# Layer 0 attention: the probabilities times v as fp32 matmuls, v kept in fp32, low halves of rows and attention made on GpSimd

## What is computed

```
def _L0_xattn_ref(q, k, v, w_q, b_q, w_k, b_k, w_v, b_v, w_o, b_o):
    qh = _split_heads(q @ w_q.T + b_q)
    kh = _split_heads(k @ w_k.T + b_k)
    vh = _split_heads(v @ w_v.T + b_v)
    scores = jnp.einsum('bhqd,bhkd->bhqk', qh, kh) / jnp.sqrt(jnp.float32(d_k))
    attn = jax.nn.softmax(scores, axis=-1)
    out = jnp.einsum('bhqk,bhkd->bhqd', attn, vh)
    return out.transpose(0, 2, 1, 3).reshape(B, S, H * d) @ w_o.T + b_o

x = x + jnp.tanh(g_xattn[0]) * _L0_xattn_ref(_layernorm(x, axis=-1), ctx_1024, ctx_1024, ...)
```

## Time and profile before

| | |
|---|---|
| median of 3 runs | 3130.3 us (3129.72 to 3131.92) |
| span of the profiled execution, first to last instruction | 3124.2 us |
| median less that span | 6.1 us |
| TensorE busy, matmul / weight load | 2797.3 us (90%) / 2225.3 us (71%) |
| VectorE, ScalarE, GpSimd busy | 2640.9 us (85%), 1875.0 us (60%), 2190.1 us (70%) |
| projection stage, about | 0 to 525 us |
| attention of layer 0, about | 527 to 1325 us |

### The profile page before, as it was taken

The page is one execution under the profiler, slowest core; times in us unless marked ns, Lnnn a source line. Parts: engine busy times, 40 slices in busy tenths (PEclk is TensorE's granted clock), DMA queues, the critical chain, the costliest instruction groups (busy, mean ns, idle before and its releaser), DMA issues.

```text
span 3124.2 us, 101333 instructions
## 1 busy us (share of the span) xinstructions
PE 2797.3 (90%) x33450; PEld 2225.3 (71%) x33450; DVE 2640.9 (85%) x6703; ACT 1875.0 (60%) x3733; POOL 2190.1 (70%) x3924
## 2 busy tenths in 40 slices
PE   4889896788888888869899999999999999999997
PEld 2444444666666666647688888888888888888886
DVE  6887886888888888875699999998989988999986
ACT  2666765777777777775455545555545555555553
POOL 3892001666667666645488888888888888888887
PEclk9999998999999999989999999999999999999999
DMA  5987666232223222623444444444444344444441
GB/s 153 361 332 289 244 243 227 73 86 79 73 78 83 80 74 77 224 82 81 96 104 111 107 101 95 104 104 95 101 91 97 94 103 104 96 98 93 108 94 43
DMA packets 367621, 388.79 MB, mean 124 GB/s; under 512 B 118432, under 2 KB 341264, under 8 KB 362320
## 3 DMA queue, kind: packets, MB, share of 16 engines
q1 hardware_dynamic: 346960, 335.42, 38.9%
q0 software_dynamic: 7328, 23.40, 2.4%
q10 hardware_dynamic: 12960, 25.23, 2.2%
HBM read 235.08 MB, written 148.83 MB: 123 GB/s over the span
## 4 chain that ended last, share of the span: by engine, by line
PE 39%; DVE 6%; issue 3%; POOL 2%; ACT 2%; DVEq 0%; POOLq 0%; ACTq 0%
PE banks L150 11%; PE banks L152 11%; PE banks L151 10%; PE banks L1310 2%; PE banks L1295 2%; DVE a_probT_lo L1397 1%; PE banks L1342 1%; ACT a_qT_hi L1199 1%; DVE a_pick L1522 1%; DVE a_y L1541 1%; DVE a_rsum L1409 1%; PE banks L1365 1%; DVE a_wsel L1531 0%; PE banks L1357 0%; ACT a_ynT_hi L1199 0%
## 5 line engine op out<-in xcount | busy, mean ns | idle before, releaser
L1199 ACT ACTIVATE a_qT_hi<-banks 128x512 f16<-128x512 f32 x252 | 150.5, 597 | 700.8 <-PE banks L152 700.8
L383 POOL TENSOR_TENSOR a_probT_lo<-a_expT,a_probT_hi 128x512 f16<-128x512 f32 (+1 forms) x384 | 372.0, 998 | 243.7 <-ACT a_probT_hi L458 243.7
L449 ACT ACTIVATE a_expT<-banks,a_top,w_score_scale 128x512 f32<-128x512 f32 (+1 forms) x384 | 272.2, 709 | 111.4 <-PE banks L544 111.2
L1112 POOL TENSOR_TENSOR a_pn<-a_prob,a_rsum 128x1024 f32<-128x1024 f32 (+1 forms) x256 | 307.2, 1221 | 5.8 <-DVE a_rsum L1411 5.3
L150 PE MATMUL banks<-a_xnT_hi,w_q_hi 128*128 128x256 f16 x1024 | 281.6, 275 | 4.7 <-DVE a_xnT_lo L1395 3.0
L150 PE MATMUL banks<-a_vo_front,a_probT_hi 128*128 128x256 f16 x1024 | 278.9, 272 | 2.7 <-DVE a_probT_lo L1397 2.6
L152 PE MATMUL banks<-a_xnT_hi,w_q_lo 128*128 128x256 f16 x1024 | 280.9, 274 | 0.0
L151 PE MATMUL banks<-a_xnT_lo,w_q_hi 128*128 128x256 f16 x1024 | 280.9, 274 | 0.0
L152 PE MATMUL banks<-a_vo_front,a_probT_lo 128*128 128x256 f16 x1024 | 279.0, 273 | 0.0
L151 PE MATMUL banks<-a_vo_front,a_probT_hi 128*128 128x256 f16 x1024 | 279.0, 272 | 0.0
L1397 DVE SCALAR_TENSOR_TENSOR a_probT_lo<-banks,a_probT_hi 128x512 f16<-128x512 f32 (+1 forms) x384 | 212.6, 582 | 35.7 <-ACT a_probT_hi L1199 35.3
(11 more groups left out here) (400 smaller groups left out, 10655.0 us busy)
## 6 DMA issues: line engine op xcount, KB each, us to landing
vo<-kv_vo_out SPq DMA_DIRECT2D x38, 2048.0 KB, 7.6
a_vo_front<-vo SPq DMA_DIRECT2D x128, 512.0 KB
kt<-kv_k_out ACTq DMA_DIRECT2D x9, 2560.0 KB, 15.0
a_k<-kt SPq DMA_DIRECT2D x64, 308.0 KB, 3.5
kv_raw_e<-in_L_ffn_w POOLq DMA_DIRECT2D x16, 1024.0 KB, 9.7
a_x<-in_x SPq DMA_DIRECT2D x64, 256.0 KB
a_y<-in_x SPq DMA_DIRECT2D x64, 256.0 KB, 2.8
x<-a_y SPq DMA_DIRECT2D x64, 256.0 KB, 2.2
```

The source lines that it names most:

```text
L383: pool.tensor_tensor(probT[b][1][0:rows, first:end, :], expT[b][0:rows, first:end, :], probT[b][0][0:rows, first:end, :], ALU.subtract).th ...
L449: act.activation(expT[1 - h][0:rows, first:end, :], bank, ACT.Exp, bias=top[0:rows, 0:1], scale=weights["score_scale"][0:rows, 0:1]).then_ ...
L1112: last = pool.tensor_tensor(keys_of(pn[h]), keys_of(prob_of(u, h, 2)), rsum[h][:, :].unsqueeze(2).broadcast_to([P, H, n]), ALU.mult)
L1199: act.activation(out, bank[:, 0:cols].rearrange("p (c s) -> p c s", c=out.shape[1]), ACT.Copy, scale=scale)\
```

## The change

v of layer 0 is stored in fp32, 17 values for a head (16 and a one) instead of 33 fp16; in the projection stage one VectorE addition writes it, and v_sum, the high copy and the low subtraction go. In attend the exponentials, fp32 and without the factor 16384, are the stationary operand of one fp32 matmul for each of the 10 chunks; the copies, the low halves on GpSimd, the bank's clearing by a zero matmul and the tile of zeros go. The buffers of the exponential are now free when the tile's att is ready. xnT and attT are evicted by ScalarE twice, in fp32 (xnT_full, attT_full) and in fp16, and GpSimd makes the low halves from these two in SBUF; VectorE's two subtractions go. Their banks are free after ScalarE's second eviction. q is still split by ScalarE and VectorE.

```diff
-    front = [sb(f"front{p}", [P, 2, 2, MAIN, 2 * head + 1], F16) for p in range(2)]
-    back = [sb(f"back{p}", [MAIN * BACK, 2, 2, MAIN, 2 * head + 1], F16) for p in range(2)]
+    front = [sb(f"front{p}", [P, 2, 2, MAIN, head + 1]) for p in range(2)]
+    back = [sb(f"back{p}", [MAIN * BACK, 2, 2, MAIN, head + 1]) for p in range(2)]
...
         if what == "xnT":
-            return xnT_ready, (i + 1) * DC + h + 1
+            return xnT_hi, (i + 1) * DC + h + 1
...
         if what == "attT":
-            return attT_ready, t - 2
+            return attT_hi, t - 2
...
-        def prob_lo(t, b):
...
+        def rows_lo(i, part):
+
+            need(pool, xnT_hi, (i + 1) * DC + part + 1)
+            pool.tensor_tensor(xnT[1][:, part, :], xnT_full[:, part, :], xnT[0][:, part, :], ALU.subtract)\
+                .then_inc(xnT_ready, 1)
+
+        def att_lo(t):
+
+            need(pool, attT_hi, t + 1)
+            pool.tensor_tensor(attT[1][:, :, :], attT_full[:, :, :], attT[0][:, :, :], ALU.subtract).then_inc(attT_ready, 1)
 
         def body(i, u, j):
             for h in range(TPB):
                 t = i * TPB + h
+                if live(t - 3, NT):
+                    att_lo(t - 3)
+                if h == 0 and live(i + 1, NB):
+                    for part in range(DC):
+                        rows_lo(i, part)
                 if h == 1 and live(i + 2, NB):
                     deviation(i + 2)
-                if live(t - 1, NT):
-                    prob_lo(t - 1, 1 - h)
                 if h == 0 and live(i, NB):
                     add_row(i, u, j)
...
                 if use[0] == "xnT":
+                    act.activation(xnT_full[:, n, :], bank, ACT.Copy)
                     act.activation(xnT[0][:, n, :], bank, ACT.Copy).then_inc(xnT_hi, 1)
...
-            need(act, prob_ready, (t - 1) * PG)
-            act.activation(expT[1 - h][0:rows, first:end, :], bank, ACT.Exp, bias=top[0:rows, 0:1],
+            need(act, att_ready, t - 1)
+            act.activation(expT[1 - h][0:rows, first:end, :], bank, ACT.Exp,
                            scale=weights["score_scale"][0:rows, 0:1]).then_inc(exp_done, 1)
...
+                    act.activation(attT_full[:, :, :], bank, ACT.Copy)
                     act.activation(attT[0][:, :, :], bank, ACT.Copy).then_inc(attT_hi, 1)
...
-            need(pe, prob_ready, (t + 1) * PG)
+            need(pe, exp_done, (t + 1) * PG)
...
+                nc.tensor.matmul(out[:, c * MAIN:(c + 1) * MAIN, :], expT[h][0:rows, MAIN + c, :],
+                                 back[p][:, e, c, :, :], start=c == 0, stop=False)
+            for c in range(MAIN):
+                last = nc.tensor.matmul(out[:, 2 * c:2 * c + 2, :], expT[h][:, c, :],
+                                        front[p][:, e, :, c % BLK * (MAIN // BLK) + c // BLK, :],
+                                        start=False, stop=c == MAIN - 1)
...
-                nc.vector.tensor_tensor(v_sum[0:m, :], full(g, ("v", a))[0:m, 0:D], bv[0:m, :], ALU.add)\
-                    .then_inc(v_sum_ready, 1)
...
+                nc.vector.tensor_tensor(v_out[p][0:m, a, :, :, 0:D // H], by_head(full(g, ("v", a))[0:m, 0:D]),
+                                        by_head(bv[0:m, :]), ALU.add).then_inc(v_ready, 1)
...
-    v = nc.dram_tensor("v", (ROWS, 2, H // 2, 2 * (D // H) + 1), F16).ap()
+    v = nc.dram_tensor("v", (ROWS, 2, H // 2, D // H + 1), FP32).ap()
```

More of the change, by code:

```diff
@@ L398, in _ @@
         pool.memset(power[:, :], -0.5).then_inc(power_set, 1)
-        pool.memset(top[:, :], math.log(PROB_TOP)).then_inc(power_set, 1)
-        pool.wait_ge(power_set, 2)
+        pool.wait_ge(power_set, 1)
         deviation(0)
-        pool.memset(zero[:, :], 0.0).then_inc(zero_set, 1)
+        for part in range(DC):
+            rows_lo(-1, part)
         deviation(1)
@@ L600, in body @@
                     filled(last, i, ("out", h))
-        pe.wait_ge(zero_set, 1)
         for h in range(2):
@@ L618, in prepare @@
             for use in prep_uses(h, part):
-                bank, n = full(i, use)[:, 0:SEQ], use[1]
-                if use[0] == "xnT":
-                    need(dve, xnT_hi, (i + 1) * DC + n + 1)
-                    nc.vector.tensor_tensor(xnT[1][:, n, :], bank, xnT[0][:, n, :], ALU.subtract).then_inc(xnT_ready, 1)
-                else:
+                if use[0] == "q":
+                    bank, n = full(i, use)[:, 0:SEQ], use[1]
                     need(dve, q_hi, (i + 1) * BLK + n + 1)
@@ L689, in body @@
                     maximum(t)
-                if live(t - 3, NT):
-                    bank = full(i, ("attT", h))[:, 0:D].rearrange("p (c s) -> p c s", c=DC)
-                    need(dve, attT_hi, t - 2)
-                    nc.vector.tensor_tensor(attT[1][:, :, :], bank, attT[0][:, :, :], ALU.subtract).then_inc(attT_ready, 1)
                 prep(0)
@@ L1855, in keys_values_phase @@
     rowsT = [pair(f"rowsT{p}", [P, DC, BANK]) for p in range(2)]
-    v_out = [sb(f"v_out{p}", [P, CH, 2, H // 2, 2 * (D // H) + 1], F16) for p in range(2)]
+    v_out = [sb(f"v_out{p}", [P, CH, 2, H // 2, D // H + 1]) for p in range(2)]
     v_ones = sem("v_ones")
@@ L1998, in _ @@
         for p in range(2):
-            pool.memset(v_out[p][:, :, :, :, 2 * (D // H):], 1.0).then_inc(v_ones, 1)
+            pool.memset(v_out[p][:, :, :, :, D // H:], 1.0).then_inc(v_ones, 1)
         pool.wait_ge(tokens_zero, 16)
@@ L2173, in body @@
                 turn(g, 1 - p)
-            for a, m in enumerate(chunks(g)):
-                need(act, v_sum_ready, g * CH + a + 1)
-                act.activation(v_out[p][0:m, a, :, :, D // H:2 * (D // H)], by_head(v_sum[0:m, :]), ACT.Copy)\
-                    .then_inc(v_hi, 1)
         first_scalar(act)
```

54 lines of the change are left out of this document (7 added, 47 removed).

## The result

The changed kernel takes 3175.2 us (median of 4 runs, 3171.6 to 3177.0) against 3130.0 for the kernel before (4 runs): ratio 1.0148, 95% interval 1.0134 to 1.0162, so 45 us slower. The forecast was 3165, in a range of 3146 to 3190.

What follows compares the result with a forecast made beforehand. No engine is full; a loop through TensorE, VectorE and ScalarE sets attention's pace. Pairs +38, projection -5.5, start and end +2: +34.5 on the 3124.2 span, 3158.7, with the median 6.1 above: 3165 us, range 3146 to 3190.

Steps and rivals of the forecast that it cites:

- What TensorE pays for an fp32 load: Attend of layer 0: 0.111 us per weight load, two loads per matmul, attend 2.24 us, +1.14 us a step.
- The four passes: Attend: fp32 priced by columns alone, 544 columns by four passes at 2.4 GHz, would be 0.91 us; the prediction rejected it.
- the rival of hidden loads: Attend: fp32 weight loads overlap and VectorE's relief counts in full, pair 10.44 us, whole 3023 us; chance 0.06.
- the balance at 0.097: Attend: loads at 0.097 us and all projection gains kept, time within 0.2% of before; chance 0.05.
- The pair of steps: Attention stage: short plus long step go from 12.11 to 12.72 us, +0.61 a pair, +38 us over 62 pairs.
- What lies beside: Attention stage: VectorE, ScalarE and GpSimd get less work; VectorE 9.4 of 12.7 us, no bound; GpSimd's low halves cost nothing.
- GpSimd could be late: Attention stage: low halves on GpSimd arrive after their reader, 0.5 us a pair more, 3196 us; with ScalarE late, chance 0.07.
- The projection stage: One addition replaces v's 1.4 us chain per chunk; gain of 4 us in early groups and 1.5 at the end, -5.5.
- what reaches TensorE of that: Projection's first three groups: excess of two stretched v_lo over 10 us of cover, 1.8 us a group, 4 us taken.
- the 1.5 us at the end: Projection's last group: v's chain ends 1.5 to 2.7 us earlier beside stores in flight; 0 to 2.7, 1.5 us taken.
- The rival of the lower clock: Attention stage: loads at 0.213 us, attend 4.3 us, pair 16.8 us, +290 us, 3455 us; chance 0.02.
- the rest of the stage's two ends: Attention stage's start and end: extra evictions, GpSimd's 0.67 for VectorE's 0.42, first attends at lower clock; +2, bounds 0 and +6.

Runs made afterwards that it cites:

- e1: Kernel before, with xnT and attT evicted twice by ScalarE and their low halves made on GpSimd, fp16 attend kept: 3125.2 us, ratio 0.9989.
- e8: e1 with the bank of xnT and attT freed after ScalarE's fp32 eviction: 3142.1 us, ratio 1.0050.
- e2: Changed kernel, with VectorE making the low halves of xnT and attT as before: 3161.9 us, ratio 1.0099; run again 3158.4 us, 1.0105.
- e7: Changed kernel, with the three-instruction chain of v back in the projection stage, a maximum as its last instruction: 3171.8 us, ratio 1.0144.
- e4: Changed kernel, with the bank of xnT and attT freed after the fp32 eviction, fp16 halves made from SBUF: 3119.2 us, ratio 0.9968.
- e3: Changed kernel, with four of the eight front matmuls left out of each attend: 3058.5 us, ratio 0.9785.
- e6: e4 with exponentials and v in single fp16 halves, low halves left out, each matmul once: 3041.2 us, ratio 0.9731.

## Why the prediction was right, and where not

**What TensorE pays for an fp32 load** was the step on which all hung, and it held: forecast 0.111 us a load and 2.24 us an attend, measured 0.112, 2.27 and 2.24, and 0.222 a matmul when eight were taken away. One leg of it was weaker than it looked: it took L1748's 0.21 us a load for the lower clock, but the windows print a granted clock of 1.00 for 7 to 15 us; what speaks for the reading is that in the fall at 699 us the turns of 128x128 go from 0.11 to 0.21 us apart. The four passes of the Trainium skill's "FP8 and Floating Point Precision" (its lines on TensorE's precision), counted by columns, gave 0.91 us; each matmul appears as two loads and two records of a pass, and 34 or 136 columns make next to no difference (0.112 and 0.114 us a load). With that the rival of hidden loads falls, and so does the balance at 0.097.

**The pair of steps.** Scores to attend was forecast at 3.24 and 3.48 and measured at 3.16 and 3.58, the rest of the step at 3.00 and measured at 3.02 and 3.00. The pair is 12.75 for 12.72, +0.63 for +0.61, and 62 of them +39 us for +38. Short step: the wait is ended by ScalarE's xnT_hi, as forecast. Long step: not by VectorE's qT_lo, as it said, but by an exponential of ScalarE behind qT_hi, which ends about as late. The short step was forecast 0.08 us too long to its attend and the long one 0.10 too short, so the pair comes out closer than its parts.

**What lies beside.** VectorE is busy 304 of 400 us, 76%, for 74% forecast, and waits for attend; no wait of TensorE for att is left; GpSimd's low halves are never waited for. That GpSimd could be late was named as a rival; it is so only where the splitting of the probabilities stays on it (e1, e8). Costing the two evictions at no more than the two subtractions was nearly right for the pair (0.08 us against e2), but the difference of the whole kernels is 14 us, the rest of it time at the lower clock.

**The projection stage**, -5.5 us, is the term that failed. Its step "what reaches TensorE of that", a cover of 10 us exceeded in three groups, and the 1.5 us at the end were worth nothing that could be told: e7 with the chain is as fast and has its first scores 0.7 to 0.9 us later, since VectorE waits about 10 us for x afterwards. As it is written the first part doesn't even come out: two v_lo of 3.3 us exceed 0.43 by 5.8 us together, which is less than the cover of 10. One more profile of before would have shown a spread of 4 us at that place, as large as the term.

**The lower clock.** The forecast took the clock as 1.00 in the stage because TensorE would stand less. It fell four times, 6 us, and cost 7 us more in the rest. The rival of the lower clock had been thought of as a state of the whole stage (+290 us) and not as a few short places. Its 3455 is also added up wrongly: +290 is already against the kernel before, and with the other two terms gives some 3417.

The sum against the spans: pairs +39 (forecast +38), the four places +6 (0), the rest of the stage's two ends +2 (+2), its start -3.6, within the spread of that place (-5.5), the remainder of the program +7 (0): +50.4 for +34.5. The 2 of the two ends is what is left over of the stage, so that it agrees says little. Every execution whose time and span are both on record takes 1.6 to 3.1 us more than its span; that the forecast could put the median 6.1 above the span, and that it is 0.6 above in the changed kernel, comes of which execution was profiled, a fast one before and a slow one after. By medians the change costs 45 us for 35 forecast: 3165 was 10 us low, not 16. That it lies inside the range is owed to the pair; the terms beside it were missed one by one, and none of the misses was large.

## What to carry to other kernels

Price an fp32 matmul by its weight loads: at the full clock 0.222 us for each stationary operand with 32 or 34 columns to multiply, and 0.23 with 136, in the rows of this case; at L1748's slower pace 128 columns cost no more than 8. With 34 columns that is dearer than three fp16 matmuls (2.25 us against 0.98 for ten operands), so here it could pay only by what else it frees. That was worth 1.9 us a pair against 2.5, and what tipped it was to release the bank after the first, exact eviction: that one reordering on ScalarE turned +45 us into -10. Take a second profile of the kernel before ahead of pricing a term of a few us from a place where a stage begins: over all profiles of this case the first scores lie between 533.0 and 542.1 us.

## What was not expected of the hardware

SyncE's queue needs about 0.5 us to issue each load of k or of v's back (3.92 us for 8, 7.89 for 16) and 0.6 to 0.7 for one of v's front, and with 34 issues in two pairs of steps it bounds the stage (where attend is cheap) at 10.56 us a pair, though the DMA engines are busy a third of the time.

The granted clock goes to 0.50 for some 3.4 us inside a stage in which TensorE is busy 97% of the time (724 of 745 us): in the changed kernel at 699, 917, 1136 and 1303 us, in its second profile within 0.3 us of the same places, in e7 at 648, 867, 1085 and 1304, in e2 three times and once. In e4, where TensorE is busy all 400 of 400 us, and in before, e1 and e3 (334 to 388 of 400 us busy) it never does between 570 and 1230 us, while in e6, with 328 of 400, it does six times between 621 and 1069 us. So TensorE's busy share does not sort these kernels. In the changed kernel each place costs 1.5 us. What starts them is open.
